# Two ScalarE squares, the seed of the roots and the order of the beginning in a float32 attention and feed-forward block

## The reference

```python
x = tokens                                   # [32, 256, 128]
xn = layernorm(x)
def attn(t):                                 # 16 heads of 64
    h = t * rsqrt(mean(t**2) + eps) * norm_w
    q, k, v = h @ Wq, *split(h @ Wkv, 2)     # 128 -> 1024 each
    q = q / max(norm(q), 1e-12) * (q_gamma + 1) * 8   # per head
    k = k / max(norm(k), 1e-12) * (k_gamma + 1) * 8
    sim = 50 * tanh(q @ k.T / 50) / 8
    return (softmax(sim) @ v) @ Wo
def ffn(t):                                  # 128 -> 512 -> 128, exact gelu
    m1, m2 = products of even and odd token rows 1..16 of the batch
    h = gelu(t @ (W1 + scale * m1).T + b1)
    return h @ (W2 + scale * m2).T + b2
out = x + attn(xn) + ffn(xn)
```

## Time and profile before

| | |
|---|---|
| time, median of 3 runs | 1115.67 us (1115.66, 1115.67, 1117.9) |
| the profiled execution | 1117.53 us, span of its instructions 1115.5 us |
| mean granted clock of TensorE | 0.995 |
| PE matmul busy | 1045.9 us, 94% |
| PE weight loads busy | 835.4 us, 75% |
| ACT busy | 1034.0 us, 93% |
| DVE busy | 931.7 us, 84% |
| POOL busy | 854.0 us, 77% |
| chain that ended last | PE 49%, ACT 23%, DVE 18%, issue 8% |

### The profile page before, as it was taken

One profiled execution on the slowest core, in us unless ns is written; L12 is line 12 of the kernel. 1 busy time (PEld: TensorE's weight loads), 2 busy tenths in 40 slices (PEclk: granted clock), 3 DMA queues, 4 the chain that ended last, 5 costly groups with the idle time before them and its releaser, 6 DMA issues.

```text
span 1115.5 us, 33883 instructions
## 1 busy us (share of the span) xinstructions
PE 1045.9 (94%) x12873; PEld 835.4 (75%) x12873; DVE 931.7 (84%) x2185; ACT 1034.0 (93%) x1543; POOL 854.0 (77%) x784
## 2 busy tenths in 40 slices
PE   3789999999999999999999999999999999999987
PEld 2557787777787777787777777777778777778776
DVE  4888898888898888889888889888889888889872
ACT  3599999999999999999999999999999999999996
POOL 5577787778788878778778778778778778778663
PEclk9899999999999999999999999999999999999999
DMA  4143343354343344443334444444335344344441
GB/s 149 40 82 68 80 85 69 73 87 73 80 81 73 74 82 76 79 80 77 77 74 79 80 80 78 73 77 80 78 79 82 69 77 87 74 79 77 70 91 30
DMA packets 310743, 86.45 MB, mean 77 GB/s; under 512 B 282036, under 2 KB 309816, under 8 KB 310584
## 3 DMA queue, kind: packets, MB, share of 16 engines
q1 hardware_dynamic: 310584, 84.30, 39.8%
HBM read 12.13 MB, written 4.19 MB: 15 GB/s over the span
## 4 chain that ended last, share of the span: by engine, by line
PE 49%; ACT 23%; DVE 18%; issue 8%; POOL 0%; ACTq 0%; POOLq 0%
PE ps_scores L492 11%; ACT probs L582 6%; ACT clamped L575 6%; PE ps_y L542 6%; PE ps_aux L467 6%; DVE qk L770 6%; PE ps_aux L426 5%; PE ps_o L520 4%; ACT L619 4%; DVE norm L685 3%; PE ps_aux L428 3%; PE ps_aux L427 3%; ACT hid L619 3%; PE ps_y L540 3%; PE ps_o L522 3%
## 5 line engine op out<-in xcount | busy, mean ns | idle before, releaser
L937 POOL TENSOR_TENSOR probs_lo<-probs 128x1024 f16<-128x1024 f32 x256 | 485.1, 1895 | 216.3 <-ACT probs L582 214.1
L575 ACT ACTIVATE clamped<-ps_scores 128x1024 f32<-128x1024 f32 x256 | 265.7, 1038 | 34.6 <-PE ps_scores L492 28.8
L582 ACT ACTIVATE probs<-clamped 128x1024 f32<-128x1024 f32 x256 | 273.3, 1067 | 2.2 <-PE ps_o L522 0.7
L520 PEld LDWEIGHTS ps_o<-v_hi,probs 128*128 128x128 bf16 x2048 | 183.9, 98 | 60.6 <-issue 58.1
L520 PE MATMUL ps_o<-v_hi,probs 128*128 128x65 bf16 x2048 | 213.8, 195 | 5.2 <-DVE newton_r L698 1.7
L492 PE MATMUL ps_scores<-heads_T 64*128 64x256 f16 x3072 | 212.8, 271 | 4.3 <-ACT clamped L575 4.2
L426 PE MATMUL ps_aux<-w_hi,xhT_hi 128*128 128x512 f32 x384 | 179.6, 468 | 38.7 <-DVE qk L770 29.1
L521 PE MATMUL ps_o<-v_lo,probs 128*128 128x64 bf16 x2048 | 211.8, 192 | 0.0
L522 PE MATMUL ps_o<-v_hi,probs_lo 128*128 128x65 bf16 x2048 | 211.4, 193 | 0.0
L521 PEld LDWEIGHTS ps_o<-v_lo,probs 128*128 128x128 bf16 x2048 | 187.3, 99 | 0.0
L522 PEld LDWEIGHTS ps_o<-v_hi,probs_lo 128*128 128x128 f16 x2048 | 187.3, 97 | 0.0
(11 more groups left out here) (80 smaller groups left out, 1927.1 us busy)
## 6 DMA issues: line engine op xcount, KB each, us to landing
heads_T<-halves SPq DMA_TRANSPOSE x512, 2.5
x_in<-in_L_attn_tokens_dram SPq DMA_DIRECT2D x32, 128.0 KB, 2.4
x_res<-in_L_attn_tokens_dram SPq DMA_DIRECT2D x32, 128.0 KB, 2.3
out_dram<-y_sb SPq DMA_DIRECT2D x32, 128.0 KB, 2.5
sel_raw<-xn SPq DMA_DIRECT2D x192, 4.0 KB
qk<-in_L_attn_Wkv_dram SPq DMA_DIRECT2D x2, 512.0 KB, 5.3
qk<-in_L_attn_Wq_dram SPq DMA_DIRECT2D x1, 512.0 KB, 3.7
qk<-in_L_ffn_W_dram SPq DMA_DIRECT2D x2, 256.0 KB
```

The lines of the kernel that those rows point to most:

```text
L520: pe.matmul(full, hi[:, col], v_hi[:, par, u, h], start=(u == 0), stop=False)
L575: nc.scalar.activation(clamped[:].rearrange("p j n -> p (j n)"), ps_scores[:].rearrange("p j n -> p (j n)"), ACT.Tanh).then_inc(clamp_done, 1)
L582: nc.scalar.activation(probs[:, pair % RING].rearrange("p j n -> p (j n)"), clamped[:].rearrange("p j n -> p (j n)"), ACT.Exp, bias=LIFT, ...
L937: g.tensor_tensor(probs_lo[:, buf].rearrange("p j n -> p (j n)"), probs[:, buf].rearrange("p j n -> p (j n)"), probs[:, buf].rearrange("p ...
```

## The change

In `SCALAR_STEPS`, the square of `("q", 3, 1)` moves ahead of tanh in step 0, and that of `("q", 0, 2)` ahead of exp in step 4. In `VECTOR_STEPS`, the product of `("q", 3, 1)` moves ahead of `divide` in step 0, and the two seed instructions move from step 2 to step 3, behind `divide` and ahead of `normalise`; the first Newton instruction moves behind `normalise`. The wait of `values` for `seed_made` in step 3 goes.

At the start, `ident` is made first on GpSimd. The gammas are loaded as 8 rows instead of 128 copies, multiplied there by VectorE (`g_rows`), and spread over the partitions by eight matmuls (`spread_gammas`), which ScalarE copies to `g_bc`. TensorE makes the first `xT` before it turns the feed-forward weights. Each third of the weights has its own wait, and the values' third comes last: its load stands behind those of W1, W2 and the second x, and its `w_lo` is made inside round -2. VectorE doesn't wait for the masks any more.

```diff
 SCALAR_STEPS = [
-    [("half", 3), ("tanh",), ("q", 3, 1), ("exp",), ("k", 2, 1), ("k", 3, 1)],
+    [("half", 3), ("q", 3, 1), ("tanh",), ("exp",), ("k", 2, 1), ("k", 3, 1)],
...
-    [("tanh",), ("exp",), ("q", 0, 2)],
+    [("tanh",), ("q", 0, 2), ("exp",)],
...
 VECTOR_STEPS = [
-    [("halves", 3), ("q", 2, 1), ("divide",), ("q", 3, 1), ("normalise",), ("result",), ("sum", 4, 1)],
+    [("halves", 3), ("q", 2, 1), ("q", 3, 1), ("divide",), ("normalise",), ("result",), ("sum", 4, 1)],
...
-    [("halves", 3), ("divide",), ("normalise",), ("sum", 7, 1), ("seed", 0), ("seed", 1), ("low", 1, 0)],
-    [("halves", 3), ("divide",), ("newton", 0), ("normalise",), ("newton", 1), ("newton", 2), ("newton", 3), ("newton", 4),
+    [("halves", 3), ("divide",), ("normalise",), ("sum", 7, 1), ("low", 1, 0)],
+    [("halves", 3), ("divide",), ("seed", 0), ("seed", 1), ("normalise",), ("newton", 0), ("newton", 1), ("newton", 2), ("newton", 3), ("newton", 4),
      ("halves", 4)],
...
+            for j, gamma in enumerate((q_gamma, k_gamma)):
+                sp.dma_start(g_raw[:, j], gamma.rearrange("(a h) d -> a (h d)", h=2)).then_inc(gammas_loaded, 16)
             sp.dma_start(w_raw[:, 0:HEADS * DH], wq).then_inc(w_loaded[0], 16)
             sp.dma_start(w_raw[:, HEADS * DH:QK], wkv[:, 0:HEADS * DH]).then_inc(w_loaded[1], 16)
-            sp.dma_start(w_raw[:, QK:QKV], wkv[:, HEADS * DH:2 * HEADS * DH]).then_inc(w_loaded[2], 16)
             sp.dma_start(w1_raw, w1.rearrange("(c p) d -> p c d", p=P)).then_inc(ffn_loaded, 16)
             sp.dma_start(w2_raw, w2).then_inc(ffn_loaded, 16)
             sp.dma_start(x_in[:, 1], tokens[1].rearrange("(t p) d -> p t d", p=P)).then_inc(x_loaded[1], 16)
+            sp.dma_start(w_raw[:, QK:QKV], wkv[:, HEADS * DH:2 * HEADS * DH]).then_inc(w_loaded[2], 16)
             sp.dma_start(b1_raw[:], b1.rearrange("(c p) -> c p", p=P)).then_inc(ffn_loaded, 16)
-            for j, gamma in enumerate((q_gamma, k_gamma)):
-                sp.dma_start(g_raw[:, j], gamma.rearrange("(o h) d -> o (h d)", o=1).to_broadcast([P, HEADS * DH]))\
-                    .then_inc(gammas_loaded, 16)
...
+            def spread_gammas():
+
+                pe.wait_ge(ident_made, 2)
+                pe.wait_ge(gammas_made, 2)
+                for a in range(PAIRS):
+                    bank, at = a // 4, a % 4 * P
+                    ins = pe.matmul(ps_scores[:, bank, at:at + P], ident[0:PAIRS, a:a + 1].to_broadcast([PAIRS, P]), g_rows[:],
+                                    start=True, stop=True)
+                ins.then_inc(gammas_spread, 1)
...
-                if s == 3:
-                    wait(pe, seed_made, min(2 * (n + 2), 2 * batches))
...
+            spread_gammas()
+            aux(first, *XT_TASK)
+            turn_ffn()
             run_all(pe, run)
...
+            weights_hi(0)
+            weights_hi(1)
+            aux(Step(-1, 0, ()), *XT_TASK[1:])
+            act.wait_ge(gammas_spread, 1)
+            for j in range(2):
+                nc.scalar.copy(g_bc[:, j * 512:(j + 1) * 512], ps_scores[:, j]).then_inc(gammas_copied, 1)
+            weights_hi(2)
             act.wait_ge(ffn_turned, 1)
...
+                    if st.number == -2 and s == 6:
+                        weights_lo(2)
...
-            dve.wait_ge(masks_made, 6)
-            dve.wait_ge(ffn_copied, 3)
             product_of_scales()
-            dve.wait_ge(gammas_made, 2)
-
+            scale_weights(0)
+            scale_weights(1)
+            weights_lo(0)
+            weights_lo(1)
+            aux(first, *XT_TASK[1:])
+            scale_weights(2)
+            dve.wait_ge(gammas_copied, 2)
             run_all(dve, run)
```

More of the change, by code:

```diff
@@ L175, in block_kernel @@
         g_bc = sb("g_bc", [P, HEADS * DH])
+        g_raw = sb("g_raw", [PAIRS, 2, P])
+        g_rows = sb("g_rows", [PAIRS, P])
         b1_raw = sb("b1_raw", [HC, P])
@@ L235, in block_kernel @@
         hid = sb("hid", [P, 2, HC, seq])
-        g_raw = hid[:].rearrange("p a c t -> p a (c t)")
         y_sb = sb("y_sb", [P, 2, TT, P])
@@ L246, in block_kernel @@
         masks_made = sem("masks_made")
+        masks_cleared = sem("masks_cleared")
         rows_cleared = sem("rows_cleared")
@@ L254, in block_kernel @@
         gammas_made = sem("gammas_made")
+        gammas_spread = sem("gammas_spread")
+        gammas_copied = sem("gammas_copied")
         x_loaded = [sem(f"x_loaded{i}") for i in range(2)]
@@ L321, in aux_index @@
             return [(what, n) for _, what, n, _ in AUX].index((kind, k))
+        XT_TASK = [(i, *task) for i, (_, *task) in enumerate(AUX) if task[0] == "xT"][0]
         def bank_of(kind, k):
@@ L428, in mm3, with turn_ffn @@
                 return pe.matmul(o, lo_l, hi_r, start=False, stop=last)
[L431 to L437, removed]
+            def spread_gammas():
[6 more added lines that the diff above has]
+                ins.then_inc(gammas_spread, 1)
+            def turn_ffn():
+                pe.wait_ge(ffn_loaded, 16 * 3)
+                pe.wait_ge(gammas_copied, 2)
+                for c in range(HC):
+                    pe.transpose(ps_scores[:, 0, c * P:(c + 1) * P], w1_raw[:, c], ident[:])
+                for c in range(HC):
+                    pe.transpose(ps_scores[:, 1, c * P:(c + 1) * P], w2_raw[:, c * P:(c + 1) * P], ident[:])
+                pe.transpose(ps_o[:, 0:HC], b1_raw[:], ident[0:HC, 0:HC]).then_inc(ffn_turned, 1)
             def aux(st, i, kind, k, ahead):
@@ L451, in aux @@
                     t, c = k // 2, k % 2 + (0 if kind == "q" else 2)
+                    if k == 0 and b == 0:
+                        pe.wait_ge(w_split, 1 if kind == "q" else 2)
                     if kind == "q" and k == 0:
-                        if isinstance(b, int) and b == 0:
-                            pe.wait_ge(w_split, 3)
                         wait(pe, xT_split, b + 1)
@@ L458, in aux @@
                 elif kind == "v":
+                    if k == 0 and b == 0:
+                        pe.wait_ge(w_split, 3)
                     t, c = k // 2, k % 2
@@ L562, in run @@
                             made += k[0]
-                        elif STAGE[k[1]] in st.stages:
+                        elif STAGE[k[1]] in st.stages and (st.number > -2 or what != "xT"):
                             aux(st, aux_index(what, k[0]), what, *k)
+            first = Step(-1, 0, stages_of(-2, batches))
+            first.before = ()
+            spread_gammas()
+            aux(first, *XT_TASK)
+            turn_ffn()
             run_all(pe, run)
@@ L634, in run, with weights_hi @@
                                 half(st, *normed)
-                        elif STAGE[k[1]] in st.stages:
+                        elif STAGE[k[1]] in st.stages and (st.number > -2 or what != "xT"):
                             aux(st, what, *k)
-            for c in range(3):
+            def weights_hi(c):
                 part = slice(c * HEADS * DH, (c + 1) * HEADS * DH)
@@ L784, in aux, with scale_weights, weights_lo @@
                         .then_inc(weff_made, 1)
+            def scale_weights(c):
+                dve.wait_ge(w_loaded[c], 32 if c == 0 else 16)
+                part = w_raw[:, c * HEADS * DH:(c + 1) * HEADS * DH]
+                v.tensor_scalar(part, part, nw_col[:, 0:1], None, ALU.mult).then_inc(w_scaled, 1)
+            def weights_lo(c):
+                part = slice(c * HEADS * DH, (c + 1) * HEADS * DH)
+                dve.wait_ge(w_hi_made, c + 1)
+                v.tensor_tensor(w_lo[:, part], w_raw[:, part], w_hi[:, part].bitcast(F32), ALU.subtract)\
+                    .then_inc(w_split, 1)
             def product_of_scales():
                 dve.wait_ge(gammas_loaded, 16 * 2)
-                v.tensor_scalar(g_raw, g_raw, 1.0, None, ALU.add).then_inc(gammas_made, 1)
+                v.tensor_scalar(g_raw[:], g_raw[:], 1.0, None, ALU.add).then_inc(gammas_made, 1)
                 dve.wait_ge(gammas_made, 1)
-                v.scalar_tensor_tensor(g_bc[:], g_raw[:, 0], DH / SOFTCLAMP, g_raw[:, 1],
+                v.scalar_tensor_tensor(g_rows[:], g_raw[:, 0], DH / SOFTCLAMP, g_raw[:, 1],
                                        ALU.mult, ALU.mult).then_inc(gammas_made, 1)
@@ L797, in run @@
                 for s in range(PAIRS):
+                    if st.number == -2 and s == 6:
+                        weights_lo(2)
+                    if st.number == 0 and s == 0:
+                        dve.wait_ge(ffn_copied, 3)
                     for what, *k in VECTOR_STEPS[s]:
@@ L833, in _ @@
             norm_var(first, 2)
[L835 to L843, removed]
-            dve.wait_ge(masks_made, 6)
-            dve.wait_ge(ffn_copied, 3)
-            product_of_scales()
-            dve.wait_ge(gammas_made, 2)
+            product_of_scales()
+            scale_weights(0)
[5 more added lines that the diff above has]
+            dve.wait_ge(gammas_copied, 2)
             run_all(dve, run)
@@ L897, in select @@
```

(7 more changed lines are left out.)

## The result

The changed kernel takes 1098.57 us (median), the kernel before 1115.66 us. The ratio is 0.9837, with a 95% interval of 0.9818 to 0.9857: 16 to 20 us faster. One of its four runs took 1142.85 us with a granted clock of 0.851 and is left out. The profiled execution took 1098.77 us, with a span of 1096.6 us; its span is 18.9 us shorter than that of before.

The account below looks back on a forecast made before the run. ScalarE was taken to set the pace from step 3 to 6, TensorE from v piece 3 to the next tanh(3). Loop 9.0 plus beginning 5.9 gave 14.9 us off 1115.67: 1100.8 us, forecast range 1097 to 1104.5, wider range 1095 to 1110.

Parts of the forecast that it names:

- Step 4 at nothing: In step 4, q0's square ahead of exp leaves ScalarE's work the same: 3.77 instead of 3.80 us to `half`, costed at nothing.
- Step 0, 0.35 per round at the seam: In step 0, q3's earlier square and product let TensorE's oT0 transpose start 0.35 us earlier per round.
- Seeds, 0.29 left at `half`: In step 3, with seeds behind divide, divide comes 0.57 us earlier, normalise follows 0.28 later, `half` gains 0.29 per round.
- lower bound of 0.07: In step 3, if divide gained only TensorE's 0.35 us, `half` would gain 0.07 us per round.
- The loop, 30 x 0.30 = 9.0 us: Over the 30 rounds with the oT0 stall, 0.30 us each gives 9.0 us; bounds 2 and 13.5 us.
- The first q product at 14.0: At the beginning, TensorE's first q product starts at 14.0 us instead of 19.92.
- The gain of the beginning, 5.9 us: The first q product comes 5.9 us earlier, bounds 3.5 and 7, and the gain should last.
- Rivals 1 and 2: 1: only the beginning gains, 1109.8 us, chance 0.13; 2: only the loop gains, 1106.7 us, chance 0.09.
- rival 5: The edits of steps 0 and 3 cancel and the start gives little: within 0.2%, chance 0.04.
- Rival 4: In step 4, the square behind Gelu forces one more table load every round: slower, 1142.4 us, chance 0.04.
- Rival 3: Divide gets its full 0.40 and TensorE's earlier step 5 start is partly kept: 0.45 us per round, 1096.3 us, chance 0.08.
- The closing chances: Chances for the whole change: faster by over 0.2% 0.92, within 0.2% 0.03, slower 0.05.

Follow-up runs that it names:

- e3_step4_only: The kernel before with only the step 4 edit, the square of q piece 0 ahead of exp; ratio to before 1.0001.
- e12_step4_back: The changed kernel with the square of q piece 0 behind exp again in step 4; ratio to the kernel before 0.9839.
- e6_q3_product_only: The kernel before with only VectorE's product of q piece 3 ahead of divide in step 0, its square left behind tanh; ratio to before 1.0001.
- e1_loop_only: The kernel before with only the step list edits (both squares, product of q piece 3, seeds) and the old beginning; ratio to before 0.9907.
- e2_begin_only: The kernel before with only the new beginning and the old step lists; ratio to before 0.9936.
- e8_busy_tensor: The kernel before with 20 more identity transposes on TensorE ahead of its first q product, into an unused bank; ratio to before 0.9980.

## Why the prediction was right

Forecast 1100.8 us, measured 1098.57, in the range of 1095 to 1110. The terms, by its own steps:

- **Step 4 at nothing.** Right and shown twice (`e3_step4_only`, `e12_step4_back`). 3.77 us from tanh to `half` was forecast, 3.81 measured, so its 0.02 per round isn't there either.
- **Step 0, 0.35 per round at the seam.** Right: 0.34 at the transpose (0.58 to 0.24), with another 0.06 behind it that the prediction did not have. With this edit alone most rounds are 0.33 us shorter, not 0.41, because VectorE then has no idle left up to `normalise` of pair 7. The prediction names VectorE as a limit only for the seeds; `e6_q3_product_only` shows what 0.27 us of standing still costs there.
- **Seeds, 0.29 left at `half`.** The mechanism was right and its sizes nearly so. `normalise` follows divide 0.28 us later, as forecast; divide comes 0.63 us earlier (0.57 forecast) and `half` 0.36 (0.29 forecast). But most of that is the gain of step 0; of the moved seeds are only 0.03 to 0.04. Alone they cost 0.05, which the lower bound of 0.07 left out: it took TensorE's 0.35 as given.
- **The loop, 30 x 0.30 = 9.0 us.** Measured: 33.23 - 32.90 = 0.33 per round in the mean, 30 x 0.33 = 10.0, 0.36 in most rounds, and 10.4 us in `e1_loop_only`. 1.0 to 1.4 us too little.
- **The first q product at 14.0.** Measured 14.47. Scaling the second third took 1.94 us and not 0.86, and the copies of the gammas ended at 12.25 and not at 11.7. The transposes of W1 and W2, which write the same banks, started 0.11 us behind them. The load behind that of b1 landed at 11.27 us, so the 11.3 for b1 fits and was no limit. In `e12_step4_back`, with the same beginning, that scaling took 0.75 us, the transposes started at 11.15 and the first q product at 13.25; its first tanh came at 41.80 all the same. The spreading matmuls took 0.47 each and were hidden, as forecast.
- **The gain of the beginning, 5.9 us.** Too small: 7.9 at the first tanh, 7.1 at the end in `e2_begin_only`. The missing term is TensorE's rate in round -2, which the prediction put at 1 us each way. It was 2.4 us one way at the transpose of the second batch, and `e8_busy_tensor` shows that occupying TensorE beforehand gives such a gain, of which 2.2 us last to the end there.
- **Sum.** 9.0 + 5.9 = 14.9 forecast, 18.2 measured (1.63% of 1115.7). Both parts were too small, so no error made good for another. Rivals 1 and 2 fall by `e1_loop_only` and `e2_begin_only`, rival 5 by the time. Rival 4 falls: there is no load ahead of the square, and the trace has 64 loads besides the first. Rival 3 was nearest in size, and its main reason was wrong: TensorE keeps nothing of step 4. The closing chances (within 0.2% 0.03, slower 0.05) do not quite match the 0.04 each of rivals 5 and 4.

## What to carry to other kernels

In a loop of engines that wait for each other, the longest wait in the view need not be on the path: here 57 us of it were worth nothing, and 18 us with one handover were worth 10. Follow one round and note at each handover who had no idle time; a wait that only moves when it is removed points to the next seam, and that was the better edit (14 us for one entry moved). An engine without idle time that hardly shows in the waits view can be what takes a gain back, as VectorE did in steps 0 to 3. Compare single rounds and not only their mean: a difference of 0.03 us per round is plain there and is lost in the times. Between two dependent instructions of a pipelined engine, put one that another engine waits for.

## What the runs showed of the hardware

- The same matmul ran at two rates while the granted clock read 1.00 in both stretches: mostly 0.42 us from start to start for 512 columns from 19.92 to 31 us before, 0.23 us in `e8_busy_tensor` from 19.99 on and in the changed kernel from 15.82 on. In the first 30 us of these traces the distance of starts shows the level, the column doesn't.
- Exp directly behind the tanh that it reads starts 1.11 us after it. With an independent copy between them, the copy starts 0.91 us after tanh and exp 0.47 later. The dependence costs ScalarE 0.2 us.
- VectorE's scaling of 128x1024 took 0.75 to 0.86 us in the kernel before and 1.94 us for the second third in the changed one, while GpSimd cleared masks. It isn't GpSimd's being busy as such: in `e12_step4_back` the same scaling took 0.75 us with GpSimd clearing `sel_raw` beside it, and there that memset took 0.86 us instead of 0.31. One of the two was long each time. The overlaps are in the traces; that they are the cause wasn't tried.
